# A four-layer spectral network on one core: the inverse column transform in 32x32 tiles, with every unit mixed first

## The reference, cut to what matters

```python
h = concatenate([x_groups, grid]); h = gconv1x1(h, fc0_w, fc0_b)
for i in range(4):
    xf = rfft2(h)                               # 24 row modes x 12 column modes are kept
    h1 = irfft2(mixed_modes(xf, sp_w1[i], sp_w2[i]))
    h2 = gconv1x1(h, w_w[i], w_b[i])            # the mixing of the channels, pixel by pixel
    h = h1 + h2
    if i < 3:
        h = gswish(h, betas[i])
h = gswish(gconv1x1(h, fc1_w, fc1_b), betas[3])
return gconv1x1(h, fc2_w, fc2_b)
```

## Time and profile before

| | us |
|---|---|
| median of three runs | 16533.06 (16531.08 to 16544.77) |
| the profiled execution | 16511.4, its span 16509.6 |
| TensorE busy in the span | 15595.9 (94%) |
| ScalarE busy | 10842.2 (66%) |
| VectorE busy | 7346.3 (44%) |

### The profile page before, as it was taken

How to read it: one execution, slowest core, us unless ns; L and a number is a source line. 1 busy time by engine, 2 the same in 40 slices (tenths; PEclk the granted TensorE clock), 3 DMA queues, 4 the chain that set the end, 5 groups by cost and what they waited for, 6 DMA issues and landing times.

```text
span 16509.6 us, 551496 instructions
## 1 busy us (share of the span) xinstructions
PE 15595.9 (94%) x240662; PEld 6399.1 (39%) x240662; DVE 7346.3 (44%) x9452; ACT 10842.2 (66%) x10628; POOL 66.7 (0%) x101
## 2 busy tenths in 40 slices
PE   4999999999999999999999999999999999999999
PEld 2334433344433444333443334443344433344333
DVE  4434543344533445434454334444344543445433
ACT  1775567766676656777666776567666677766677
POOL 0000000000000000000000000000000000000000
PEclk9999999999999999999999999999999999999999
DMA  1111111111111111111111111111111111111111
GB/s 46 44 35 45 39 41 44 36 45 40 44 41 44 38 39 43 40 46 35 45 40 40 44 37 44 39 43 42 41 40 40 42 40 47 35 44 40 40 44 36
DMA packets 512280, 679.95 MB, mean 41 GB/s; under 512 B 90930, under 2 KB 483338, under 8 KB 493718
## 3 DMA queue, kind: packets, MB, share of 16 engines
q1 hardware_dynamic: 507318, 642.77, 14.8%
q10 hardware_dynamic: 2408, 0.28, 0.0%
HBM read 507.45 MB, written 135.27 MB: 39 GB/s over the span
## 4 chain that ended last, share of the span: by engine, by line
issue 82%; PE 16%; DVE 1%; ACT 0%; POOL 0%; DVEq 0%; DMA 0%; POOLq 0%; ACTq 0%; SPq 0%
PE PS L750 5%; PE PS L761 4%; PE PS L684 2%; PE PS L692 2%; PE PS L636 1%; PE PS L590 1%; PE PS L514 1%; PE PS L619 0%; PE PS L524 0%; ACT hmem L851 0%; PE PS L655 0%; ACT work L858 0%; PE PS L615 0%; POOL mv L1214 0%; DVE work L1094 0%
## 5 line engine op out<-in xcount | busy, mean ns | idle before, releaser
L750 PE MATMUL PS<-hmem,fcw 31*128 31x512 f32 x32768 | 4452.7, 641 | 153.1 <-ACT work L858 55.1
L858 ACT ACTIVATE work<-PS 128x512 f32<-128x512 f32 (+1 forms) x4480 | 4231.0, 1028 | 340.6 <-PE PS L750 340.6
L750 PEld LDWEIGHTS PS<-hmem,fcw 31*128 31x128 f32 x32768 | 1293.3, 183 | 3260.6 <-ACT work L858 1615.6
L851 ACT ACTIVATE hmem<-PS 128x2048 f32<-128x2048 f32 x1056 | 1982.9, 1878 | 508.9 <-PE PS L692 338.0
L761 PE MATMUL PS<-work,fcw 128*32 128x512 f32 x17920 | 2188.9, 602 | 0.0
L1194 DVE SCALAR_TENSOR_TENSOR work<-PS,work 128x512 f32<-128x512 f32 x1056 | 730.4, 692 | 3131.2 <-PE PS L761 3131.2
L1123 DVE STREAM_TRANSPOSE work<-hmem 128x2048 f32<-128x2048 f32 x864 | 1910.8, 2277 | 416.2 <-ACT hmem L851 416.0
L858 ACT ACTIVATE gst<-PS 128x512 f32<-128x512 f32 (+1 forms) x2048 | 1993.9, 1037 | 2.0 <-PE PS L750 2.0
L829 ACT ACTIVATE gst<-PS 128x264 f32<-128x264 f32 x640 | 236.1, 423 | 2607.1 <-PE PS L615 1584.4
L858 ACT ACTIVATE hmem<-PS 128x512 f32<-128x512 f32 (+1 forms) x1664 | 1613.2, 1021 | 202.7 <-PE PS L750 195.1
L692 PE MATMUL PS<-invc,gst 24*128 24x256 f32 x22528 | 1535.5, 402 | 1.3 <-issue 1.3
(11 more groups left out here) (141 smaller groups left out, 11105.8 us busy)
## 6 DMA issues: line engine op xcount, KB each, us to landing
work<-in_x SPq DMA_DIRECT2D x1518, 128.0 KB, 2.5
wspec<-in_spec_w SPq DMA_DIRECT2D x768, 90.0 KB, 2.1
hmem<-x_d SPq DMA_DIRECT2D x128, 528.0 KB
x_d<-work SPq DMA_DIRECT2D x512, 128.0 KB, 2.9
wspec<-in_spec_w SPq DMA_DIRECT2D x768, 60.0 KB, 2.0
fcw<-fcw_d SPq DMA_DIRECT2D x32, 960.0 KB, 5.3
work<-x_d SPq DMA_DIRECT2D x384, 64.0 KB
wspec<-x_d SPq DMA_DIRECT2D x384, 64.0 KB
```

The lines of the kernel that those rows point to most:

```text
L750: mm = nc.tensor.matmul(PS[:, fc_bank(p, r), :], f1w[32 * r:32 * r + 31, k, g, :], hmem[32 * r:32 * r + 31, g * PART + u * ROW2:g * PART + ...
L851: nc.scalar.activation(unit(u), PS[:, at:at + 4, :], ACT.Silu).then_inc(s_hrow, 1)
L858: nc.scalar.activation(act(p)[:, strips, :], PS[:, bank:bank + (3 if rest else 1), :], ACT.Silu).then_inc(s_silu, 1)
```

## The change

Each of the 8 products of `inverse_columns` is cut into four, one for each 32 output columns `q`, so that it runs in the same 32x32 tiles as the mixing: 32 products of 256 columns a unit. All units now mix first, and the inverse transform always adds to what is there. The semaphore moves with the last product.

```diff
 def inverse_columns(u, at, first):
     for y in range(2):
-        for r in range(4):
-            mm = nc.tensor.matmul(PS[:, at + r, y * W:y * W + W],
-                                  gst[32 * r:32 * r + MODES, 2 * u + y, :, :].rearrange("p s o -> p (s o)"),
-                                  invc[32 * r:32 * r + MODES, :], start=first and y == 0, stop=not first,
-                                  tile_position=(32 * r, 0), skip_group_check=True)
+        for q in range(4):
+            for r in range(4):
+                mm = nc.tensor.matmul(PS[32 * q:32 * q + 32, at + r, y * W:y * W + W],
+                                      gst[32 * r:32 * r + MODES, 2 * u + y, q, :],
+                                      invc[32 * r:32 * r + MODES, :], start=first and y == 0, stop=not first,
+                                      tile_position=(32 * r, 32 * q), skip_group_check=True)
     return mm
...
         pe.sem_inc(s_bank, 1)
-        if u % 2 == 0:
-            mix(lay, u, at, True)
+        mix(lay, u, at, True)
         if u == 0:
...
-        mm = inverse_columns(u, at, u % 2 == 1)
-        if u % 2 == 1:
-            mm = mix(lay, u, at, False)
-        mm.then_inc(s_row, 1)
+        inverse_columns(u, at, False).then_inc(s_row, 1)
```

## The result

The changed kernel takes **17503.36 us**, median of four runs (17492.92 to 17515.68), against 16536.47 us for the kernel before in the same comparison: a ratio of **1.0584** (95% interval 1.0569 to 1.0599), 967 us slower. The prediction was 17433.

What follows compares the result with a forecast made beforehand. TensorE bounds the kernel, busy 94%; the changed one starves for instructions. Pixel stages add 27.7 us an image, +886 over 32 images, row transforms +15: about +900 on the profiled 16511, carried to 17433 us; range 17037 to 17800.

Steps and rivals of the forecast that it cites:

- TensorE starved for instructions: Pixel stages: 192 instructions a unit outrun the packet supply, so a unit takes 2.92 us; chance 0.87.
- The counts: Whole kernel: 96 instructions a unit become 192, 135,168 added in all; some 2500 instruction packets, 41 MB.
- The interval: Instruction queue: a starved TensorE gets one packet of 247 instructions every 3.75 us, between 3.5 and 4.0.
- Layers 0 to 2: Pixel stages of the first three layers: 24.1 us each become 30.8, 6.7 more in each.
- The last layer: Its pixel stage: 23.2 us become 30.8, 7.6 us more an image.
- a pixel stage of 30.8 us in every layer: Pixel stages: 8.5 packets, 7.5 intervals of 3.75 us plus 1.35 us at each end, the same in all layers.
- always in time: Pixel stages of the kernel before: their instruction packets never come late; cited in favour of the faster rival.
- The row transforms: After pixel stages: each begins without a packet in hand, 0 to 1.2 us in 96 stages, 0 to +115, taken +15.
- The array: Inverse transform in small tiles: four rounds take 0.88 to 1.10 us against 1.02 before, 0.08 lost to 0.14 gained a unit.
- these waits go: Weight loader between mixing and inverse transform: idle times of 0.84 and 0.33 us vanish with one tile shape.
- instructions in time: Rival, pixel stages: packets arrive early enough, ScalarE's 2.05 us sets the unit, 183 us less, 16350 us; chance 0.08.
- That rival: Pixel stages: holes drop TensorE's clock to its lower level, units of some 3.4 us, 18200; chance 0.02 shared with turns.

Runs made afterwards that it cites:

- after_late: Changed kernel with the last layer's loads (dense weights, first two residuals) held back until ten of its eleven units are through: 17519.14 us, ratio 1.0613 to the kernel before.

## Why the prediction was right, and where it was off

**The bound.** TensorE starved for instructions was the mechanism, and it is shown three ways: more instructions for the same work cost 3.56 us a packet, less work for the same instructions changed nothing, and two thirds of the instructions put layers 0 to 2 back to within 0.35 us of where they were.

**The counts** came out: 192 instructions a unit, about 2500 packets and 41 MB predicted, 2478 and 40.60 measured. I reckoned with 247 instructions a packet, TensorE's records over all packets; the added ones show 256. With 256 and the measured 3.83 us a unit would be 192 / 256 x 3.83 = 2.87 us in place of my 2.92; ScalarE's mean step in layers 0 to 2 is 2.87. The two errors, 247 for 256 and 3.75 for 3.83, partly cancel.

**The interval.** I took 3.75 us from three packets around one hole, with bounds of 3.5 and 4.0. Measured in layers 0 to 2 it is 3.79 to 3.87, and 3.69 to 3.77 with 320 instructions a unit. This was the open cost, and the nearest row, though only 7.5 us long, had the answer.

**Layers 0 to 2.** Predicted 30.8 us a stage and 6.7 more than before, 20.1 for three; measured 30.75, 31.83 and 30.74, and 20.19 more for three. That the sum agrees to 0.1 is partly luck: both kernels' stages are 0.3 us longer on the mean than I had put. Singly they differ, since the kernel before is not 24.1 in each. Its layer 0 is 25.03 on the mean: 11 of the 32 stages had a stretch at the 1.2 GHz level and took 27.3 us, the other 21 took 23.8, and the one I had cut is of these.

**The last layer is the term that was mis-sized.** I put 30.8 there as elsewhere, against 23.2, so 7.6 us an image. It is 34.58 against 24.69, so 9.89. The missing 2.29 us an image are 73 us in all, and the prediction was 70 short. The step that failed is "a pixel stage of 30.8 us in every layer": I took the clean interval from a stretch in which the other queues are silent and carried it to one in which they are not. With loads at 119 GB/s beside it a packet came late and left a hole of 4.82 us, and in 15 of the 32 images the clock fell as well. The last layer of the kernel before, whose loads show in its stretch already as 62 GB/s, should have made me ask; that the packets of its pixel stages "are always in time" was wrong, for its six long last stages have loader holes of 2.7 to 4.5 us. `after_late` shows that it is the loads: 30.58 without them, the figure that I had put there.

**The row transforms.** I gave them 15 us. The spans leave 987 - 963 = 24 us for all that lies outside the pixel stages, and the traces separate it. From the last product of a pixel stage to the last one of `columns` behind it took 12.73, 12.78 and 12.68 us in layers 0, 1 and 2 before, as a mean over 32 images, and 13.18, 12.79 and 13.70 after: 1.48 us an image, 47 us in all. So this term was too small as well, inside its bounds of 0 to 115. From the last pixel stage of an image to the first of the next one the changed kernel is 0.97 us quicker, some 30 us, for which I had put nothing and know no reason; by luck it makes up for the 32 us that were missing here.

**The array.** I had bounded the inverse transform in small tiles by 0.88 and 1.10 us. Both were too low, which starving hid. At the start of one layer 0 the changed kernel runs four units with instructions in hand (ScalarE, then the weight loader of the middle one):

```profile
8388.87 1.88 ACT L848 ACTIVATE hmem<-PS 128x2048 f32<-128x2048 f32 x1 [0.45 <-PE PS L693]
8391.19 1.88 ACT L848 ACTIVATE hmem<-PS 128x2048 f32<-128x2048 f32 x1 [0.44 <-PE PS L693]
8393.51 1.88 ACT L848 ACTIVATE hmem<-PS 128x2048 f32<-128x2048 f32 x1 [0.44 <-PE PS L693]
```

```profile
8389.43 1.24 PEld L693 LDWEIGHTS PS<-invc,gst 24*32 24x32 f32 x63 [0.33 <-issue]
8390.86 0.44 PEld L684 LDWEIGHTS PS<-hmem,compw 28*32 28x32 f32 x32 [0.20 <-issue]
8391.33 0.10 PEld L693 LDWEIGHTS PS<-invc,gst 24*32 24x32 f32 x1
8391.75 1.24 PEld L693 LDWEIGHTS PS<-invc,gst 24*32 24x32 f32 x63 [0.33 <-issue]
```

A unit is an even 2.32 us, not ScalarE's 2.05: the 63 loads take 1.24 us and the step from mixing to inverse transform still leaves the loader idle for 0.33 and 0.20, though all tiles have one shape. I had said that these waits go; only 0.84 + 0.33 became 0.33 + 0.20. So my rival "instructions in time" had the wrong price and sign: at 2.32 against 2.19 it would give 0.13 x 1408 = 183 us more, not 183 less. That is worked out from these rows and not run; by it, the change would have been slower with instructions in time too. The rows also show that TensorE can take instructions faster than they come: 192 in 2.32 us is 256 in 3.1 us, less than the 3.75 of the floor.

**What else I set aside.** The clock did fall behind a hole, to 0.50 at 8584, and in the last layer it did so more often than before: 15 of the 32 stages had a stretch at the 1.2 GHz level, against 5. In layers 0 to 2, with their holes of about 1 us, it did not: 13 of 96 stages had such a stretch, against 17 before. In the whole run the lower level takes 494 us after and 523 before (mean granted clock 0.986 and 0.984). That rival was right about its mechanism in the last layer and wrong about its size.

**The rule on the page.** The Trainium skill, in "Runtime: NRT & Kernel Launch", section "Instruction fetch mechanics", calls the crossing of a block of 256 instructions "mostly hidden". The runs agree up to 128 instructions in 2.2 us and disagree beyond: 3.56 us for each block more.

## What to carry to other kernels

Count an edit's instructions as well as its columns: divide the instructions between two waits by the time that they take, and compare it with the fastest stretch in which the kernel already runs dry (here 256 in 3.75 us, 15 ns each). A single hole of one microsecond that comes back at the same place of the program, with nothing named as its end, can hold the price of a whole change. And take a price only to stretches with the same neighbours: beside bulk loads the same packet came several microseconds late.

## What the runs showed of the hardware

- One block of 256 instructions for TensorE takes about 3.75 us when the next is wanted at once (3.69 to 3.87 in the stages of three kernels without bulk loads beside them). Reading from the rows, only one is under way at a time; no run shows the mechanism itself.
- An instruction packet comes late beside bulk loads: up to 10.0 us after the one before it, a hole of 4.82 us with 119 GB/s beside it, and a stage 4.0 us shorter without the loads. It is the packet's beginning that is late; its own transfer takes 1.1 us on the mean with the loads and without.
- Small tiles of 24 rows, 256 columns a product, took 1.24 us for 63 loads, 20 ns each; with 128 columns 63 loads still took 0.99 us, as the loader of the run with half the columns shows:

```profile
8432.54 0.99 PEld L693 LDWEIGHTS PS<-invc,gst 24*32 24x32 f32 x63 [0.33 <-issue]
```

Halving the columns saved a fifth. So part of the cost of a set of small products does not go with their columns, which I had not expected from the row transform's rounds of 0.275 us.
